# First graph of a graph-convolution kernel: x loaded transposed, centred and scaled from banks that TensorE fills

## The chip, the core and the metric

The kernel runs on one core of one Trainium2 chip. The metric is the device time of one execution in microseconds (us). A core has TensorE (PE in the profile; its weight loads are PEld), VectorE (DVE), ScalarE (ACT), GpSimd (POOL) and SyncE (SP), each with its own queue of instructions taken in order. They wait for each other by semaphores. Data lie in SBUF; TensorE writes to PSUM, of which this kernel uses eight banks of 128 partitions x 512 floats: `u_ps0` to `u_ps3` and `rot_ps0` to `rot_ps3`.

## The reference, cut to what matters

16 graphs, each with 512 nodes of 384 features. Before the two layers the features are normalised and clipped; this is the step that the change rewrites for the first graph.

```python
h = jnp.maximum(_layernorm(x, axis=-1), 0.0)       # (x - mean) / sqrt(var + 1e-5)
# per layer, on h of shape (B, 512, 384):
u = jnp.einsum('bid,bjd->bij', h, h) / temper
a = jax.nn.softmax(u, axis=-1)
delta = a * adjacency_matrix
attn = delta / (jnp.sum(delta, axis=-1, keepdims=True) + 1e-10)
hl, hs, hr = h @ wl.T + b_l, h @ ws.T + b_s, h @ wr.T + b_r
ctx = (attn * upper) @ hl + diag_a[..., None] * hs + (attn * lower) @ hr
o = relu((ctx - mean) / jnp.sqrt(var + LN_EPS) * g + beta)
# result: x + o of the second layer
```

## The kernel before

The graphs are worked in eight pairs. A pair has four steps: layer 0 of graph a and of graph b, then layer 1 of both. In each step TensorE makes the scores of four row tiles (`scores`, or `first_scores` in the very first step), twelve projections (`project`) and four attention products (`attend`). Every product of two fp32 matrices is made of three in a rounded format: each operand is split into a high part, which ScalarE rounds, and a low part, the difference, which VectorE or GpSimd subtracts (`ht_hi`/`ht_lo` for the features, `w_hi`/`w_lo` for the weights, `hw_hi`/`hw_lo` for the projections, `et_hi`/`et_lo` for the masked exponentials). The features are held transposed, with the 384 features in three blocks (KB = 3) of 128 partitions and the 512 nodes along the free dimension.

All orders are written out by hand, one program for each engine. From the second graph on, x comes to SBUF twice: by rows into `x_norm` (`load_stat_rows`), for VectorE's mean and variance, and transposed into `xt_sb` (`load_xt`). The mean and the reciprocal deviation of the 512 rows are written to a small tensor in DRAM and read back spread over 128 partitions (`store_x_rows`, `spread_x_rows`). GpSimd subtracts the mean (`x_centre`, L924), VectorE clips and scales (`x_scale`, L670), ScalarE rounds (`round_x`, L550) and VectorE subtracts the low part (`x_low`, L728).

The first graph goes another way, since nothing can hide it. Its x is loaded by rows in four pieces of 192 KB (L274, L488). VectorE makes the statistics (L615, L621, L625), GpSimd the reciprocal deviation (`x_rstd_of`, L917), VectorE the shift (L630). ScalarE and VectorE normalise two row tiles each in place (L479, L634). TensorE, which has worked off five products on zeros until then (L349), transposes twelve 128x128 blocks into three banks (L355). ScalarE clips and rounds each bank into `ht_hi` (L493) and VectorE takes the low part from the same bank (L645). `first_scores` begins with the first block of 128 features and waits for `ht_lo_done` once per block.

Beside this the first layer's weights are loaded in three chunks (L250), rounded by ScalarE (`round_w`, L485) and split by GpSimd (chunk 0, L932) and VectorE (chunks 1 and 2, L650). The first projection waits until all three are split. VectorE then goes on to the statistics of the second graph (`x_stats_of(1)`) and from there to the first step's evacuations (`evacuate`, L717) and masks (`mask`, L682, after ScalarE's exponential, L512). At the end of the first step GpSimd splits the first chunk of the second layer's weights (`split_w`, L937).

## Time and profile before

| | us |
|---|---|
| median of 3 runs | 1180.22 |
| lowest and highest | 1179.71, 1180.55 |
| the profiled execution's own time | 1179.74 |
| its span, first to last instruction | 1178.0 |
| TensorE busy | 1167.0 (99%) |
| VectorE, ScalarE, GpSimd busy | 939.7, 495.0, 639.4 |
| TensorE's share of the chain that ended last | 97% |

The profile comes from one execution, so durations and sums are made against its time; the 1.7 us between span and time lie outside the recorded instructions. TensorE's ends are modelled from starts and shapes. A wait is given as the idle time of an engine and the instruction that ended it. TensorE is the engine at the end of the chain for nearly the whole span; the other engines matter where it waits for them.

### The profile page before, as it was taken

How to read it: one execution, taken by the hardware profiler on the slowest of the kernel's cores; microseconds unless marked ns; L12 is line 12 of the kernel's file. 1: busy time of each engine (PE TensorE's matmuls, PEld its weight loads, DVE VectorE, ACT ScalarE, POOL GpSimd, SP SyncE). 2: the span in 40 equal slices, each digit the busy share in tenths (PEclk: the TensorE clock that was granted, in tenths of full speed). 3: DMA queues.
4: the chain of work that ended last, by engine and by line, in shares of the span. 5: the costliest groups of instructions: out<-in, count | busy, mean ns of one | idle time of the engine just before them, and what ended most of it. 6: DMA issues, size and time to landing. Idle time of an engine off the chain costs nothing.

```text
span 1178.0 us, 18565 instructions
## 1 busy us (share of the span) xinstructions
PE 1167.0 (99%) x6998; PEld 1158.1 (98%) x6998; DVE 939.7 (80%) x1872; ACT 495.0 (42%) x1065; POOL 639.4 (54%) x669
## 2 busy tenths in 40 slices
PE   9999999999999999999999999999999999999997
PEld 7999999999999999999999999999999999999997
DVE  6778986689866988769887598876988769875688
ACT  5346433364343543444334443344333454335532
POOL 4685463654635556445555456554475544754347
PEclk9999999999999999999999999999999999999999
DMA  7521312013121131211212112211212113110000
GB/s 245 187 66 55 116 55 81 22 52 117 55 81 37 36 117 55 81 37 62 91 55 81 37 68 85 67 68 37 88 66 81 55 36 113 41 54 1 1 28 27
DMA packets 43481, 80.55 MB, mean 68 GB/s; under 512 B 6912, under 2 KB 24832, under 8 KB 43392
## 3 DMA queue, kind: packets, MB, share of 16 engines
q1 hardware_dynamic: 43104, 78.98, 20.1%
q8 instruction: 55, 0.90, 0.3%
q10 hardware_dynamic: 288, 0.39, 0.1%
q14 instruction: 34, 0.28, 0.1%
HBM read 66.72 MB, written 12.64 MB: 67 GB/s over the span
## 4 chain that ended last, share of the span: by engine, by line
PE 97%; DVE 2%; issue 0%; DMA 0%; ACT 0%; POOL 0%; DVEq 0%
PE rot_ps L344 17%; PE rot_ps L343 17%; PE rot_ps L342 17%; PE u_ps L342 14%; PE u_ps L344 14%; PE u_ps L343 14%; PE rot_ps L405 2%; PE u_ps L398 2%; PE rot_ps L414 1%; DVE xt_sb L670 0%; DMA x_norm<-x_dram 0%; DVE hs L774 0%; DVE z L754 0%; DVE stats L780 0%; DVE x_stats L615 0%
## 5 line engine op out<-in xcount | busy, mean ns | idle before, releaser
L950 POOL TENSOR_TENSOR hw_lo<-proj,hw_hi 128x384 fp32r<-128x384 f32 x256 | 281.6, 1120 | 280.3 <-ACT hw_hi L530 280.3
L342 PE MATMUL rot_ps<-w_hi,ht_hi 128*128 128x384 f32 x1152 | 389.2, 338 | 0.0
L344 PE MATMUL rot_ps<-w_hi,ht_lo 128*128 128x384 f32 x1152 | 385.4, 335 | 0.0
L343 PE MATMUL rot_ps<-w_lo,ht_hi 128*128 128x384 f32 x1152 | 385.2, 334 | 0.0
L343 PEld LDWEIGHTS rot_ps<-w_lo,ht_hi 128*128 128x128 f32 x1152 | 216.5, 188 | 0.0
L342 PEld LDWEIGHTS rot_ps<-w_hi,ht_hi 128*128 128x128 f32 x1152 | 216.5, 188 | 0.0
L344 PEld LDWEIGHTS rot_ps<-w_hi,ht_lo 128*128 128x128 f32 x1152 | 216.2, 188 | 0.0
L505 ACT ACTIVATE u_off<-u_ps 128x128 f32<-128x128 f32 (+1 forms) x128 | 42.5, 332 | 393.7 <-PE u_ps L344 393.5
L717 DVE TENSOR_TENSOR proj<-rot_ps,bias 128x384 f32<-128x384 f32 x256 | 140.1, 550 | 47.4 <-PE rot_ps L344 45.7
L962 POOL TENSOR_TENSOR dg<-et_hi,tri 128x256 fp32r<-128x256 f32 x128 | 113.5, 887 | 94.5 <-PE u_ps L344 94.5
L530 ACT ACTIVATE hw_hi<-proj 128x384 fp32r<-128x384 f32 x256 | 127.9, 520 | 66.0 <-DVE proj L717 66.0
L342 PE MATMUL u_ps<-hw_hi,et_hi 128*128 128x386 f32 x384 | 131.8, 343 | 0.0
L774 DVE SCALAR_TENSOR_TENSOR hs<-hs,e_diag,u_ps 128x385 f32<-128x385 f32 x128 | 78.6, 614 | 66.2 <-PE u_ps L344 65.4
L687 DVE TENSOR_TENSOR et_lo<-e_sb,et_hi 128x512 fp32r<-128x512 f32 x128 | 130.6, 1029 | 0.0
L344 PE MATMUL u_ps<-hw_hi,et_lo 128*128 128x386 f32 x384 | 129.9, 338 | 0.0
L343 PE MATMUL u_ps<-hw_lo,et_hi 128*128 128x384 f32 x384 | 129.6, 337 | 0.0
L962 POOL TENSOR_TENSOR dg<-et_lo,tri 128x256 fp32r<-128x256 f32 x128 | 120.4, 941 | 0.0
L342 PE MATMUL u_ps<-ht_hi 128*128 128x256 f32 (+1 forms) x384 | 118.8, 309 | 1.2 <-DVE ht_lo L645 0.7
L344 PE MATMUL u_ps<-ht_hi,ht_lo 128*128 128x256 f32 (+1 forms) x384 | 118.8, 309 | 0.0
L343 PE MATMUL u_ps<-ht_lo,ht_hi 128*128 128x256 f32 (+1 forms) x384 | 118.3, 308 | 0.0
L967 POOL TENSOR_TENSOR rstd<-var_eps,minus_half 128x4 f32<-128x4 f32 (+1 forms) x35 | 38.7, 1105 | 124.3 <-DVE var_eps L741 123.9
L717 DVE TENSOR_TENSOR hs<-rot_ps,bias 128x384 f32<-128x384 f32 x128 | 67.0, 549 | 26.7 <-PE rot_ps L344 26.1
(89 smaller groups left out, 2038.7 us busy)
## 6 DMA issues: line engine op xcount, KB each, us to landing
out_dram<-z SPq DMA_DIRECT2D x64, 192.0 KB, 1.9
x_norm<-x_dram SPq DMA_DIRECT2D x15, 768.0 KB, 4.3
xt_sb<-x_t_dram SPq DMA_DIRECT2D x15, 768.0 KB, 4.5
adj_a<-adj_t_dram SPq DMA_DIRECT2D x8, 1024.0 KB, 5.4
adj_b<-adj_t_dram SPq DMA_DIRECT2D x8, 1024.0 KB, 5.4
x_norm<-rows_dram SPq DMA_DIRECT2D x15, 512.0 KB, 3.8
x_a<-x_dram SPq DMA_DIRECT2D x8, 768.0 KB, 4.6
x_b<-x_dram SPq DMA_DIRECT2D x8, 768.0 KB, 4.6
```

Of the source, the lines that this page charges most:

```text
L342: pe.matmul(dst, a_hi, b_hi, start=first and m == 0, stop=False)
L343: pe.matmul(dst[:, 0:b_lo.shape[1]], a_hi, b_lo, start=False, stop=False)
L344: done = pe.matmul(dst, a_lo, b_hi, start=False, stop=last and m == n - 1)
L398: done = pe.transpose(u_ps[t][:, column * P:(column + 1) * P], u_off[:, source * P:(source + 1) * P], ident[:, :])
L505: act.activation(u_off[:, OFF_AT[t] * P:OFF_AT[t] * P + width], u_ps[t][:, first_block * P:first_block * P + width], ACT.Copy).then_inc(of ...
L530: act.activation(hw_hi[:, t, n, 0:dim], proj[:, t % 2, n, :], ACT.Copy).then_inc(hw_hi_done, 1)
L687: dve.tensor_tensor(et_lo[:, i, :], e_sb[:, i, :], et_hi[:, i, :].bitcast(F32), ALU.subtract).then_inc(et_lo_done, 1)
L717: dve.tensor_tensor(dst, bank(it, s, "P", t, n)[:, 0:dim], bias[:, layer, n, :], ALU.add).then_inc(p_freed, 1)
L774: dve.scalar_tensor_tensor(out=hs[:, i, 0:dim + 1], in0=hs[:, i, 0:dim + 1], scalar=e_diag[:, i:i + 1], in1=u_ps[i][:, 0:dim + 1], op0=ALU ...
L950: pool.tensor_tensor(hw_lo[:, t, n, :], proj[:, t % 2, n, :], hw_hi[:, t, n, 0:dim].bitcast(F32), ALU.subtract).then_inc(hw_lo_done, 1)
L962: pool.tensor_tensor(dg[:, i % 2, part, :, :], block_t.unsqueeze(1).to_broadcast([P, 2, P]), tri[:, :, :], ALU.mult).then_inc(dg_done, 1)
L967: pool.tensor_tensor(rstd[:, cols], var_eps[:, cols], minus_half[:, cols], ALU.pow).then_inc(rstd_done, 1)
```

## The change

The first graph's x is now loaded twice, by rows for the statistics as before, and transposed into `xt_sb` right behind (one DMA of 768 KB, ahead of the weights in SP's queue). Normalising by rows, the shift and the twelve transposes of x are gone. In their place TensorE spreads the mean: four transposes of a broadcast column of `x_mv` fill bank `rot_ps1` so that every partition holds the 512 means, and four more fill `rot_ps2` with the reciprocal deviations. VectorE subtracts bank 1 from a block of `xt_sb` (`centre_first`), clips and multiplies by bank 2 (`scale_first`), ScalarE rounds the block from SBUF, and VectorE subtracts the rounded part, from SBUF too (`low_first`). ScalarE's rounding of the first weight chunk moves behind the first block's. The load of the second graph's rows waits for the first graph's statistics instead of its transposes, and that of its transposed x for the first graph's three low parts. The other edits renumber waits whose semaphores now count the first graph as well.

```diff
@@ -168,9 +167,7 @@
         ht_lo_done = sem("ht_lo_done")
         x_stats_done = sem("x_stats_done")
         x_rstd_done = sem("x_rstd_done")
-        x_shift_done = sem("x_shift_done")
-        x_norm_act_done = sem("x_norm_act_done")
-        x_norm_dve_done = sem("x_norm_dve_done")
+        x_first_spread = sem("x_first_spread")
         ones_done = sem("ones_done")
         stats_done = sem("stats_done")
         aggr_done = sem("aggr_done")
...
@@ -272,12 +268,14 @@
 
             for t in range(0, TILES, 2):
                 sp.dma_start(x_norm[:, t, :], rows(x, 0)[:, t, :]).then_inc(x_first[t], 16)
+            load_xt(0)
             for c in range(KB):
                 load_w(c)
             load_bias(0)
             sp.dma_start(adj_sb[0][:, :, :], rows(adj_t, 0)).then_inc(adj_loaded[0], 16)
-            sp.wait_ge(t_ready, KB)
+            sp.wait_ge(x_stats_done, TILES)
             load_stat_rows(1)
+            sp.wait_ge(ht_lo_done, KB)
             load_xt(1)
             sp.dma_start(gamma_t[:, :], ln_w0_t[:, :]).then_inc(col_loaded, 16)
             sp.dma_start(beta_t[:, :], ln_b0_t[:, :]).then_inc(col_loaded, 16)
...
@@ -294,7 +292,7 @@
             def pair(it, first, last):
                 next_a, next_b = it * 2 + 2, it * 2 + 3
                 if not last:
-                    sp.wait_ge(xt_scaled, KB * (next_a - 1))
+                    sp.wait_ge(xt_scaled, KB * next_a)
                     load_stat_rows(next_a)
                     sp.wait_ge(ht_lo_done, LEAD_T + at(it, 0, KB, N_H))
                     load_xt(next_a)
...
@@ -313,7 +311,7 @@
                     sp.wait_ge(w_lo1_done, KB)
                     sp.dma_start(x_sb[1][:, :, :], rows(x, 1)).then_inc(x_loaded[1], 16)
                 if not last:
-                    sp.wait_ge(xt_scaled, KB * next_a)
+                    sp.wait_ge(xt_scaled, KB * next_b)
                     spread_x_rows(next_b)
                 for g in range(2):
                     s = 2 + g
...
@@ -348,13 +346,16 @@
             for _ in range(5):
                 pe.matmul(rot_ps[0][:, :], diag_junk[:, 0, :], flat(diag_junk, 0, n_rows), start=True, stop=True)
             pe.wait_ge(consts, 8)
-            pe.wait_ge(x_norm_dve_done, TILES - X_ACT)
-            pe.wait_ge(x_norm_act_done, X_ACT)
-            for db in range(KB):
+            def spread_first(q):
                 for t in range(TILES):
-                    done = pe.transpose(rot_ps[(db - KB) % ROT][:, t * P:(t + 1) * P],
-                                        x_norm[:, t, db * P:(db + 1) * P], ident[:, :])
-                done.then_inc(t_ready, 1)
+                    done = pe.transpose(rot_ps[1 + q][:, t * P:(t + 1) * P],
+                                        x_mv[:, 0, q, t:t + 1].to_broadcast([P, P]), ident[:, :])
+                done.then_inc(x_first_spread, 1)
+
+            pe.wait_ge(x_stats_done, 2 * TILES)
+            spread_first(0)
+            pe.wait_ge(x_rstd_done, 1)
+            spread_first(1)
 
             def step(it, s, first, last):
                 final = last and s == STEPS - 1
...
@@ -473,12 +474,6 @@
 
         @block.scalar
         def _(act):
-            def x_normalise_first():
-                act.wait_ge(x_shift_done, 1)
-                for t in range(X_ACT):
-                    act.activation(x_norm[:, t, :], x_norm[:, t, :], ACT.Identity, bias=x_shift[:, t:t + 1],
-                                   scale=x_mv[:, 0, 1, t:t + 1]).then_inc(x_norm_act_done, 1)
-
             def round_w(c):
                 layer, kb = chunks[c]
                 act.wait_ge(w_loaded[c], 16)
...
@@ -486,11 +481,11 @@
 
             for t in range(1, TILES, 2):
                 act.dma_start(x_norm[:, t, :], rows(x, 0)[:, t, :]).then_inc(x_first[t], 16)
-            x_normalise_first()
-            round_w(0)
             for db in range(KB):
-                act.wait_ge(t_ready, db + 1)
-                act.activation(ht_hi[:, 0, db, :], rot_ps[(db - KB) % ROT][:, :], ACT.Relu).then_inc(ht_hi_done, 1)
+                act.wait_ge(xt_scaled, db + 1)
+                act.activation(ht_hi[:, 0, db, :], xt_sb[:, db, :], ACT.Copy).then_inc(ht_hi_done, 1)
+                if db == 0:
+                    round_w(0)
             for c in range(1, KB):
                 round_w(c)
 
...
@@ -544,13 +539,13 @@
 
                 def round_x(db):
                     graph = it * 2 + (1 if s == 0 else 2)
-                    act.wait_ge(xt_scaled, KB * (graph - 1) + (db + 1))
+                    act.wait_ge(xt_scaled, KB * graph + (db + 1))
                     if s == 2 and db == 0:
                         act.wait_ge(p_ready, at(it, s, 3 * TILES, N_P))
                     act.activation(ht_hi[:, graph % 2, db, :], xt_sb[:, db, :], ACT.Copy).then_inc(ht_hi_done, 1)
 
                 def round_h(db):
-                    act.wait_ge(t_ready, LEAD_T + at(it, s, db + 1, N_HT))
+                    act.wait_ge(t_ready, at(it, s, db + 1, N_HT))
                     src, parity = bank(it, s, "T", db)[:, :], 1 - s % 2
                     if db == 0:
                         act.wait_ge(hw_lo_done, at(it, s, 2 * TILES, EIGHT))
...
@@ -625,26 +620,37 @@
                 dve.tensor_scalar(x_var_eps[:, :], x_mv[:, graph % 2, 1, :], 1e-5, None,
                                   ALU.add).then_inc(x_stats_done, 1)
 
-            def x_normalise_first():
-                dve.wait_ge(x_rstd_done, 1)
-                dve.scalar_tensor_tensor(out=x_shift[:, :], in0=x_mv[:, 0, 0, :], scalar=-1.0, in1=x_mv[:, 0, 1, :],
-                                         op0=ALU.mult, op1=ALU.mult).then_inc(x_shift_done, 1)
-                dve.wait_ge(x_shift_done, 1)
-                for t in range(X_ACT, TILES):
-                    dve.tensor_scalar(x_norm[:, t, :], x_norm[:, t, :], x_mv[:, 0, 1, t:t + 1], x_shift[:, t:t + 1],
-                                      ALU.mult, ALU.add).then_inc(x_norm_dve_done, 1)
+            def centre_first(db):
+                dve.tensor_tensor(xt_sb[:, db, :], xt_sb[:, db, :], rot_ps[1][:, :],
+                                  ALU.subtract).then_inc(xt_centred, 1)
+
+            def scale_first(db):
+                dve.wait_ge(xt_centred, db + 1)
+                dve.scalar_tensor_tensor(out=xt_sb[:, db, :], in0=xt_sb[:, db, :], scalar=0.0, in1=rot_ps[2][:, :],
+                                         op0=ALU.max, op1=ALU.mult).then_inc(xt_scaled, 1)
+
+            def low_first(db):
+                dve.wait_ge(ht_hi_done, db + 1)
+                dve.tensor_tensor(ht_lo[:, 0, db, :], xt_sb[:, db, :], ht_hi[:, 0, db, :].bitcast(F32),
+                                  ALU.subtract).then_inc(ht_lo_done, 1)
 
             dve.memset(diag_junk[:, :, :], 0.0).then_inc(zeros_done, 1)
             for t in range(TILES):
                 dve.wait_ge(x_first[t], 16)
                 x_statistics(t)
             x_variance(0)
-            x_normalise_first()
-            for db in range(KB):
-                dve.wait_ge(ht_hi_done, db + 1)
-                dve.scalar_tensor_tensor(out=ht_lo[:, 0, db, :], in0=rot_ps[(db - KB) % ROT][:, :], scalar=0.0,
-                                         in1=ht_hi[:, 0, db, :].bitcast(F32), op0=ALU.max,
-                                         op1=ALU.subtract).then_inc(ht_lo_done, 1)
+            dve.wait_ge(x_first_spread, 1)
+            dve.wait_ge(xt_loaded, 16)
+            centre_first(0)
+            centre_first(1)
+            dve.wait_ge(x_first_spread, 2)
+            scale_first(0)
+            scale_first(1)
+            low_first(0)
+            centre_first(2)
+            scale_first(2)
+            low_first(1)
+            low_first(2)
             for c in range(1, KB):
                 dve.wait_ge(w_hi_done, c + 1)
                 dve.tensor_tensor(w_lo[:, 0, c, :], w_stages[c], w_hi[:, 0, c, :].bitcast(F32),
...
@@ -666,7 +672,7 @@
 
                 def x_scale(graph, db):
 
-                    dve.wait_ge(xt_centred, KB * (graph - 1) + (db + 1))
+                    dve.wait_ge(xt_centred, KB * graph + (db + 1))
                     dve.scalar_tensor_tensor(out=xt_sb[:, db, :], in0=xt_sb[:, db, :], scalar=0.0, in1=rstd_b,
                                              op0=ALU.max, op1=ALU.mult).then_inc(xt_scaled, 1)
 
...
@@ -918,7 +924,7 @@
                                    ALU.pow).then_inc(x_rstd_done, 1)
 
             def x_centre(graph):
-                pool.wait_ge(xt_loaded, 16 * graph)
+                pool.wait_ge(xt_loaded, 16 * (graph + 1))
                 pool.wait_ge(x_rows_spread, 16 * graph)
                 for db in range(KB):
                     pool.tensor_tensor(xt_sb[:, db, :], xt_sb[:, db, :], mean_b, ALU.subtract).then_inc(xt_centred, 1)
```

In the first rows of TensorE's queue (rot_ps0 to rot_ps3 are the banks, diag_junk the zeros) there stands before:

```order
L349 MATMUL rot_ps0<-diag_junk 128x512 [waits zeros_done]
L349 MATMUL rot_ps0<-diag_junk 128x512 x4
L355 MATMUL rot_ps1<-ident,x_norm 128x128 [waits x_norm_act_done,x_norm_dve_done,consts]
L355 MATMUL rot_ps1<-ident,x_norm 128x128 x3
L355 MATMUL rot_ps2<-ident,x_norm 128x128 x4
L355 MATMUL rot_ps3<-ident,x_norm 128x128 x4
L342 MATMUL u_ps0<-ht_hi 128x384 [waits ht_lo_done]
```

and in the changed kernel, whose line numbers differ by a few:

```order
L347 MATMUL rot_ps0<-diag_junk 128x512 [waits zeros_done]
L347 MATMUL rot_ps0<-diag_junk 128x512 x4
L351 MATMUL rot_ps1<-ident,x_mv 128x128 [waits x_stats_done,consts]
L351 MATMUL rot_ps1<-ident,x_mv 128x128 x3
L351 MATMUL rot_ps2<-ident,x_mv 128x128 [waits x_rstd_done]
L351 MATMUL rot_ps2<-ident,x_mv 128x128 x3
L340 MATMUL u_ps0<-ht_hi 128x384 [waits ht_lo_done]
```

Eight small transposes of statistics take the place of twelve of x; both sets stand behind the same five products on zeros.

VectorE's queue between the first graph's variance and the second graph's statistics, before (x_mv holds mean and variance, w_lo the low weights):

```order
L625 TENSOR_SCALAR x_var_eps<-x_mv 128x4 [waits x_stats_done]
L630 SCALAR_TENSOR_TENSOR x_shift<-x_mv 128x4 [waits x_rstd_done]
L634 TENSOR_SCALAR x_norm<-x_norm,x_mv,x_shift 128x384 [waits x_shift_done]
L634 TENSOR_SCALAR x_norm<-x_norm,x_mv,x_shift 128x384
L645 SCALAR_TENSOR_TENSOR ht_lo<-rot_ps1,ht_hi 128x512 [waits ht_hi_done]
L645 SCALAR_TENSOR_TENSOR ht_lo<-rot_ps2,ht_hi 128x512 [waits ht_hi_done]
L645 SCALAR_TENSOR_TENSOR ht_lo<-rot_ps3,ht_hi 128x512 [waits ht_hi_done]
L650 TENSOR_TENSOR w_lo<-z,w_hi 128x1152 [waits w_hi_done]
L650 TENSOR_TENSOR w_lo<-x_b,w_hi 128x1152 [waits w_hi_done]
L615 BN_STATS x_stats<-x_norm 128x6 [waits consts,x_norm_loaded,zeros_done,w_lo0_done]
```

and after:

```order
L620 TENSOR_SCALAR x_var_eps<-x_mv 128x4 [waits x_stats_done]
L624 TENSOR_TENSOR xt_sb<-xt_sb,rot_ps1 128x512 [waits xt_loaded,x_first_spread]
L624 TENSOR_TENSOR xt_sb<-xt_sb,rot_ps1 128x512
L629 SCALAR_TENSOR_TENSOR xt_sb<-xt_sb,rot_ps2 128x512 [waits xt_centred,x_first_spread]
L629 SCALAR_TENSOR_TENSOR xt_sb<-xt_sb,rot_ps2 128x512 [waits xt_centred]
L634 TENSOR_TENSOR ht_lo<-xt_sb,ht_hi 128x512 [waits ht_hi_done]
L624 TENSOR_TENSOR xt_sb<-xt_sb,rot_ps1 128x512
L629 SCALAR_TENSOR_TENSOR xt_sb<-xt_sb,rot_ps2 128x512 [waits xt_centred]
L634 TENSOR_TENSOR ht_lo<-xt_sb,ht_hi 128x512 [waits ht_hi_done] x2
L656 TENSOR_TENSOR w_lo<-z,w_hi 128x1152 [waits w_hi_done]
L656 TENSOR_TENSOR w_lo<-x_b,w_hi 128x1152 [waits w_hi_done]
```

Six operations on 512 columns are new on VectorE ahead of the weights' low parts, and the three low parts of the features now read two tensors of SBUF where they read a bank and one tensor.

ScalarE's queue at the same place, before:

```order
L479 ACTIVATE x_norm<-x_norm,x_shift,x_mv 128x384 [waits x_shift_done]
L479 ACTIVATE x_norm<-x_norm,x_shift,x_mv 128x384
L485 ACTIVATE w_hi<-e_sb 128x1152 [waits w_loaded_0]
L493 ACTIVATE ht_hi<-rot_ps1 128x512 [waits t_ready]
L493 ACTIVATE ht_hi<-rot_ps2 128x512 [waits t_ready]
L493 ACTIVATE ht_hi<-rot_ps3 128x512 [waits t_ready]
L485 ACTIVATE w_hi<-z 128x1152 [waits w_loaded_1]
```

and after:

```order
L486 ACT_TABLE_LOAD
L486 ACTIVATE ht_hi<-xt_sb 128x512 [waits xt_scaled]
L480 ACTIVATE w_hi<-e_sb 128x1152 [waits w_loaded_0]
L486 ACTIVATE ht_hi<-xt_sb 128x512 [waits xt_scaled] x2
L480 ACTIVATE w_hi<-z 128x1152 [waits w_loaded_1]
```

The rounding of the first weight chunk (`w_hi<-e_sb`, which GpSimd's split waits for) has moved from ahead of the three feature blocks to between the first and the second.

## Rows read from the trace of the kernel before

**Rows 1.** Waits of TensorE, whole run: waited for, us in total, times, longest.

```profile
PE rot_ps L349 <- DVE diag_junk L637: 1.5, 1, 1.5
PE u_ps L342 <- DVE ht_lo L645: 0.7, 1, 0.7
PE u_ps L342 <- DVE ht_lo L728: 0.5, 1, 0.5
PE rot_ps L355 <- ACT x_norm L479: 0.4, 1, 0.4
```

**Rows 2.** Chain that ended last, its beginning: start us, us, what.

```profile
6.84 1.05 POOL x_mv L917
...
10.98 0.70 DVE ht_lo L645
...
11.73 0.44 PE u_ps L342
```

**Rows 3.** Timeline of TensorE and its weight loads: start us, us, instruction.

```profile
6.78 0.34 PEld L349 LDWEIGHTS rot_ps<-diag_junk 128*128 128x128 f32 x1 [0.52 <-issue]
7.63 0.24 PEld L349 LDWEIGHTS rot_ps<-diag_junk 128*128 128x128 f32 x1 [0.52 <-issue]
8.11 0.19 PEld L349 LDWEIGHTS rot_ps<-diag_junk 128*128 128x128 f32 x1 [0.24 <-issue]
...
9.56 1.50 PE L355 MATMUL rot_ps<-ident,x_norm 128*128 128x128 f32 x12 [0.43 <-ACT x_norm L479]
...
13.60 0.34 PE L342 MATMUL u_ps<-ht_hi 128*128 128x384 f32 x1
...
17.11 0.34 PE L342 MATMUL rot_ps<-w_hi,ht_hi 128*128 128x384 f32 x1
```

**Rows 4.** Timeline of the other engines, 10 to 21 us.

```profile
10.55 2.67 POOL L932 TENSOR_TENSOR w_lo<-e_sb,w_hi 128x1152 fp32r<-128x1152 f32 x1 [2.67 <-ACT w_hi L485]
...
10.98 1.89 DVE L645 SCALAR_TENSOR_TENSOR ht_lo<-rot_ps,ht_hi 128x512 fp32r<-128x512 f32 x3 [2.00 <-ACT ht_hi L493]
...
14.35 1.34 DVE L650 TENSOR_TENSOR w_lo<-x_b,w_hi 128x1152 fp32r<-128x1152 f32 x1
17.46 1.94 DVE L615 BATCH_NORM_STATS2 x_stats<-x_norm 128x6 f32<-128x384 f32 x4 [1.76 <-DMA x_norm<-x_dram]
...
19.93 0.56 DVE L717 TENSOR_TENSOR proj<-rot_ps,bias 128x384 f32<-128x384 f32 x1
20.40 0.68 DVE L682 TENSOR_TENSOR e_sb<-u_ps,adj_a 128x512 f32<-128x512 f32 x1
...
19.53 0.58 ACT L512 ACTIVATE u_ps<-u_ps 128x512 f32<-128x512 f32 x1 [1.94 <-PE u_ps L398]
```

**Rows 5.** Groups by line and shape, whole run: count, busy us, mean ns, idle before.

```profile
L687 DVE TENSOR_TENSOR et_lo<-e_sb,et_hi 128x512 fp32r<-128x512 f32 x128 | 130.6, 1029 | 0.0
...
L550 ACT ACTIVATE ht_hi<-xt_sb 128x512 fp32r<-128x512 f32 x45 | 26.4, 625 | 52.8 <-DVE xt_sb L670 52.8
```

**Rows 6.** GpSimd's split beside VectorE (timeline); L728 over the run: min/median/max ns.

```profile
43.89 2.66 POOL L937 TENSOR_TENSOR w_lo<-x_b,w_hi 128x1152 fp32r<-128x1152 f32 x1
...
44.36 2.74 DVE L728 TENSOR_TENSOR ht_lo<-xt_sb,ht_hi 128x512 fp32r<-128x512 f32 x1
...
L728 DVE TENSOR_TENSOR ht_lo<-xt_sb,ht_hi x45: 678/684/2736, 42.5 to 1057.4; 128x512 fp32r<-128x512 f32 x45
```

**Rows 7.** Two weight DMAs: issue in SP's timeline; then KB, us to landing.

```profile
1.69 0.42 SPq L250 DMA_DIRECT2D e_sb<-w_t_dram  x1
2.16 0.43 SPq L250 DMA_DIRECT2D z<-w_t_dram  x1
...
e_sb<-w_t_dram SPq DMA_DIRECT2D x1, 576.0 KB, 5.1
z<-w_t_dram SPq DMA_DIRECT2D x1, 576.0 KB, 6.2
```

**Rows 8.** Busy time by engine, 27 to 46 us, with counts; granted clock, DMA.

```profile
27.00:46.00 19.00, 19.00 (x111) 19.00 (x110) 16.03 (x22) 5.22 (x9) 19.00 (x17) 1.00 0.62 221
```

2 lines of the change are left out of this document (removed).

## The prediction

> **What bounds the kernel now.** I read the view of waits first, for TensorE over the whole run. It has four entries [rows 1]: 1.5 us until its first operand, 0.4 us for the normalised x before the opening transposes, 0.7 us for the first `ht_lo`, and 0.5 us for an `ht_lo` of the second graph (L728). Behind those TensorE is fed to the end. So the kernel ends when TensorE has done a fixed amount of work, and a change in the first graph's preparation counts only by what it does to the start of the first scores, now 11.73 us, and to stalls behind it. The chain of waits gives the way to that start [rows 2]: GpSimd's reciprocal deviation is there at 7.89, VectorE's first `ht_lo` runs from 10.98, the first score at 11.73. In the timeline TensorE is not free all that time [rows 3]. The five opening products on zeros are ten passes of 512 columns. Their weight loads come 0.85 us apart up to 7.63 (the lower of the two clock levels, 1.2 GHz) and 0.48 us apart there (2.4 GHz), although the profile's clock column grants 1.00 throughout. The last pass starts about 0.43 us after the load at 8.11 and streams for 0.43 us, so the engine is free at about 8.97. Before, this cost nothing: the transposes waited for ScalarE until 9.5 anyway.
>
> **Edits with one answer.** The shift, two ScalarE normalisations, two on VectorE and twelve transposes go. The renumbered waits (`xt_scaled`, `xt_centred`, `xt_loaded`, `t_ready`) only count the first graph's increments too, which costs nothing in steady state. SP's queue issues one DMA more, so the seven behind it are issued some 0.45 us later.
>
> **The load of x transposed.** It stands ahead of the weights in SP's queue. The second weight block was issued at 2.16 and landed 6.2 us later, at 8.36, when 0.79 MB of x and 1.18 MB of weights had moved [rows 7]. The transposed x needs 0.79 + 0.79 MB moved, less than that, so I take about 7.3 and at most 8.4. Nothing wants it before 9.6: free. If that cover were gone, each late microsecond would be one. The two weight blocks landed 1.57 us apart for 0.59 MB, 375 GB/s, so 0.79 MB delays what lies behind by 2.1 us. The first weights then land near 8.9, wanted at 12.0. The second graph's x for its statistics, which ended VectorE's wait at 17.46 [rows 4], lands near 19.5. Its issue moved ahead (it now waits for the statistics, about 6.2), but the queue is full until then.
>
> **The start of the first scores.** The spreads stand behind the opening products. Twelve transposes took 1.50 us, 0.112 us each and 0.27 us the last [rows 3], so the mean's bank is full at 8.97 + 0.34 + 0.27 = 9.58 and the other at 10.03, both later than their data (about 6.6 and 7.89). VectorE is not shown subtracting a bank from SBUF at this size. The nearest rows are the mask on a bank, 0.68 us long, and the old `ht_lo`, three in 1.89 us, one every 0.60 [rows 4]. I take 0.60 from start to start and 0.68 for the last; the ends would be 0.5 and 0.7, for the sum some 0.3 us either way. Two centrings start at 9.60 and 10.20, the first scaling runs 10.80 to 11.48. ScalarE's copy of a 128x512 block of SBUF takes 0.63 us on average [rows 5]: 12.13. `low_first(0)` ends at 12.83, the scores start at 12.88. That is **1.15 us later** than 11.73.
>
> **The second block.** Block 0 of the scores takes 13.60 − 11.73 = 1.87 us [rows 3], so TensorE wants `ht_lo` of block 1 at 14.75. In the new order ScalarE rounds the first weights between `ht_hi` 0 and 1 (1.15 us, 12.05 to 13.20), and then GpSimd splits them, 13.20 to 15.87, if it takes its 2.67 us [rows 4]. VectorE does centring 2 (12.75), scaling 2 (13.45) and wants `low_first(1)` at about 14.05. Before, this subtraction read a bank: it ran beside the same GpSimd split at full speed (10.98 against 10.55) [rows 4]. Now both of its inputs lie in SBUF. The trace has that pair once: GpSimd's split of other weights from 43.89 for 2.66 us, VectorE's `ht_lo` from SBUF at 44.36 for 2.74 us, where the median of 45 such is 0.68 [rows 6]. It ended 0.55 us behind the split, so it did nothing until the split was over. By that row `low_first(1)` ends at 15.87 + 0.55 = 16.42 and TensorE goes on at 16.47, where it was at 13.60: **2.87 us later**, 1.72 of it a new stall.
>
> The mean of 128 `et_lo` subtractions beside shorter GpSimd work is 1.03 us [rows 5], which could be read as a slowdown by half instead: the subtraction would end near 15.1 and TensorE be 1.5 us late. The Trainium skill (SBUF — State Buffer, section SBUF: two separate sides) says that the port pair of VectorE and GpSimd is an exclusive lock for a whole instruction, taken by a VectorE operation with two SBUF inputs against a GpSimd one that reads SBUF. By that rule the sum is the 2.87 above, by the other reading about 1.5; the row at 44.36 agrees with the rule.
>
> **Behind the scores.** Blocks 1 and 2 take 17.11 − 13.60 = 3.51 us: first projection at 19.98. It waits for all first low weights. VectorE has `ht_lo` 2 done at 17.05 and then two splits of 1.34 us [rows 4], done at about 19.65: 0.3 us to spare. VectorE's statistics of the second graph follow, from 19.65 (data at 19.5). Before, 2.47 us passed from their start to the first evacuation, 17.46 to 19.93: now 22.1, or 2.2 late. But the first mask waits for ScalarE's first exponential, which follows TensorE's mirrors, so it moves from 19.53 to 22.41, ends 0.58 later, and the mask starts at 23.03 where it started at 20.40: 2.63 late [rows 4]. Evacuations, rounding and GpSimd's lower parts follow that by 2.63 us. GpSimd is busy for all 19 us from 27 to 46 [rows 8], so it brings this lateness to the split at 43.89 and the `ht_lo` behind it, for which TensorE waits 0.5 us [rows 1, 6]. TensorE comes there 2.87 late, GpSimd 2.63: the stall shrinks from 0.5 to about 0.3, and all that follows is **2.6 us late**. Its floor, with the stall gone, is 2.87 − 0.5 = 2.4; if GpSimd were as late as TensorE, 2.9.
>
> **The sum.** Span 1178.0 + 2.6 = 1180.6; the profiled execution took 1179.74 and would take 1182.4. It lies 0.5 under the median 1180.22, from which the forecast is **1182.8 us**. With 0.3 for VectorE's steps and 0.3 for the floor, its own range is 1182.1 to 1183.5.
>
> **Rivals.**
> - *VectorE is not held by GpSimd* (20%). If `low_first(1)` ends by about 15.1, by sharing or by coming first, no long stall appears. TensorE is 1.2 to 1.5 late, the low weights about 1.9 at worst: 1181.5 to 1182.1, say 1181.9, not slower by more than can be told. It decides at about 15.2 us. For it: the margin between 13.20 and 14.05 is only 0.85 us, and the 1.03 us rows. Against it: the 2.74 us row.
> - *The chain gets shorter as the words of the change suggest* (7%). If the opening products ended before the data came (the clock rising sooner), the banks would be full at 7.2 and 8.5, the scores would start near 10.6, 1.2 early. But the split then runs about 10.9 to 13.6 and `low_first(1)` ends at 14.1 against 13.60 before: 0.5 late, 1180.8. To be faster by 0.2% it would have to gain 2.4 us, more than this start plus the later stall (1.7) can give.
> - *TensorE's clock falls* (13%). It would work 1 us between 9 and 12.9 and wait again at 14.75. At the lower level a pass takes 0.85 instead of 0.43 us [rows 3]. The first block's loss hides in the new stall; behind 16.47 the loss is half of the slow time. At the start it took about 6 us of work before the clock rose, so from 16.5 it stays low until 19 to 22.5: 1.3 to 3 us more, 1183.9 to 1185.8, say 1184.8. For it: 4.5 of these 6.5 us are idle. Against it: 1.1 us idle before the old start left the pitch at the upper level. The Trainium skill (TensorE: Matmul & The Clock Gate, section What's actually happening) says that the throttled state is the default and activity releases it; that a gap of this size is enough to bring it back no run here shows.
>
> **How the numbers follow.** Forecast 60%, rivals 20, 7 and 13%. A run of this kernel can tell about 0.2% (2.4 us), so slower means above 1182.6: of the forecast's 60 some 42 points, and all 13 of the clock: 55% slower. Same: 18 + 20 + 5: 43%. Faster 2%. The range 1180.9 to 1184.6 takes in forecast, the first rival and part of the others.
>
> **What the changed profile would show.** The mean's spread starts at 9.0, behind the zeros' products, not at 6.6. First score at 12.9. `low_first(1)` is over 2 us long and ends 0.55 behind GpSimd's first split; TensorE has a new wait of about 1.7 us for it. The wait at L728's counterpart near 50 us is 0.2 to 0.5. A `low_first(1)` of 0.7 us, a start before 12 or score passes at twice the pitch would each prove a step wrong, as would VectorE waiting for the transposed x.

## The result, and the profile after

The changed kernel takes **1184.14 us** (median of 8 runs, 1182.12 to 1184.60), the kernel before 1179.91 in the 8 runs made beside them (1179.71 to 1180.57). The ratio is 1.0029, 95% interval 1.0020 to 1.0039. It is slower, as forecast, and inside the stated range. It is 1.3 us above the predicted time, and beyond the forecast's own range of 1182.1 to 1183.5. The profiled execution took 1184.05 with a span of 1182.3, 4.3 more than before.

TensorE's waits answer to [rows 1] (waited for, us in total, times, longest):

```profile
PE u_ps L340 <- DVE ht_lo L634: 3.8, 2, 2.9
PE rot_ps L347 <- DVE diag_junk L637: 1.5, 1, 1.5
PE u_ps L340 <- DVE ht_lo L734: 0.5, 1, 0.5
```

The wait for the first graph's `ht_lo` grew from 0.7 to 3.8 us in two pieces, and the wait in the second graph (L728 before, L734 now) is still 0.5. So all 4.3 us arise before the first projection, the first product that needs the weights. The timeline of TensorE shows where (start us, us, instruction, idle before it and its releaser), beside [rows 3]:

```profile
1.50 6.98 PE L347 MATMUL rot_ps<-diag_junk 128*128 128x512 f32 x10 [1.50 <-DVE diag_junk L637]
8.32 1.04 PE L351 MATMUL rot_ps<-ident,x_mv 128*128 128x128 f32 x8
12.28 0.44 PE L340 MATMUL u_ps<-ht_hi 128*128 128x384 f32 x1 [2.93 <-DVE ht_lo L634]
...
15.90 0.69 PE L340 MATMUL u_ps<-ht_hi 128*128 128x384 f32 x1 [0.83 <-DVE ht_lo L634]
...
21.39 0.34 PE L340 MATMUL rot_ps<-w_hi,ht_hi 128*128 128x384 f32 x1
```

The first score is 0.55 us later than before (12.28 for 11.73), the second block 2.30 later (15.90 for 13.60), the first projection 4.28 later (21.39 for 17.11). The last step, from 2.30 to 4.28, is blocks 1 and 2 taking 5.49 us instead of 3.51. The windows of 2 us say why (busy us and count of each engine, then PEclk, DMA share, GB/s):

```profile
12.00:14.00 2.00, 1.72 (x8) 1.72 (x9) 1.97 (x4) 1.50 (x3) 1.36 (x1) 0.81 0.87 123
14.00:16.00 2.00, 1.17 (x7) 0.87 (x5) 2.00 (x2) 2.00 (x3) 1.30 (x1) 0.50 0.95 333
16.00:18.00 2.00, 2.00 (x7) 2.00 (x8) 2.00 (x3) 0.32 (x1) 0.00 (x0) 0.50 1.05 426
18.00:20.00 2.00, 2.00 (x10) 2.00 (x10) 0.99 (x1) 0.00 (x0) 0.00 (x0) 0.50 1.02 352
20.00:22.00 2.00, 2.00 (x15) 2.00 (x14) 0.59 (x2) 1.30 (x4) 0.00 (x0) 0.99 0.52 175
```

Here the granted clock falls to 0.50, the 1.2 GHz level, at about 13.3 us and comes back at about 20. In TensorE's weight loads it is the step from 0.19 to 0.33 us:

```profile
13.09 0.19 PEld L342 LDWEIGHTS u_ps<-ht_hi,ht_lo 128*128 128x128 f32 x1
13.27 0.33 PEld L340 LDWEIGHTS u_ps<-ht_hi 128*128 128x128 f32 x1
```

They are back at 0.19 at 20.16. Ahead of the fall TensorE had done 1.04 us of small transposes, idled 2.93 us and worked about 1 us on the scores.

The other engines, VectorE's and GpSimd's timelines, answer to [rows 4]:

```profile
8.96 1.28 DVE L624 TENSOR_TENSOR xt_sb<-xt_sb,rot_ps 128x512 f32<-128x512 f32 x2 [2.30 <-PE rot_ps L351]
10.16 1.28 DVE L629 SCALAR_TENSOR_TENSOR xt_sb<-xt_sb,rot_ps 128x512 f32<-128x512 f32 x2
11.54 0.69 DVE L634 TENSOR_TENSOR ht_lo<-xt_sb,ht_hi 128x512 fp32r<-128x512 f32 x1
...
13.46 2.99 DVE L634 TENSOR_TENSOR ht_lo<-xt_sb,ht_hi 128x512 fp32r<-128x512 f32 x2
...
21.41 1.94 DVE L610 BATCH_NORM_STATS2 x_stats<-x_norm 128x6 f32<-128x384 f32 x4 [2.42 <-DMA x_norm<-x_dram]
...
24.60 0.69 DVE L688 TENSOR_TENSOR e_sb<-u_ps,adj_a 128x512 f32<-128x512 f32 x1 [0.17 <-ACT u_ps L507]
```

```profile
12.64 2.67 POOL L938 TENSOR_TENSOR w_lo<-e_sb,w_hi 128x1152 fp32r<-128x1152 f32 x1 [4.86 <-ACT w_hi L480]
```

The subtraction of the second block of features ends at 15.86 (the chain of waits gives it from 13.55 for 2.31), 0.55 us behind the end of GpSimd's split at 15.31. And a second thing is late: the second graph's statistics start at 21.41, 3.95 us later than 17.46, still ended by their rows' DMA.

SP's issues and the DMAs' times to landing (KB, us) answer to [rows 7]:

```profile
1.69 0.43 SPq L257 DMA_DIRECT2D xt_sb<-x_t_dram  x1
2.16 0.49 SPq L246 DMA_DIRECT2D e_sb<-w_t_dram  x1
...
5.69 0.64 SPq L275 DMA_DIRECT2D adj_a<-adj_t_dram  x1
6.37 2.30 SPq L254 DMA_DIRECT2D x_norm<-x_dram  x1
```

```profile
adj_a<-adj_t_dram SPq DMA_DIRECT2D x1, 1024.0 KB, 13.7
xt_sb<-x_t_dram SPq DMA_DIRECT2D x1, 768.0 KB, 6.9
x_norm<-x_dram SPq DMA_DIRECT2D x1, 768.0 KB, 14.9
e_sb<-w_t_dram SPq DMA_DIRECT2D x1, 576.0 KB, 7.8
```

The added load lands at 8.6, just ahead of its use at 8.96. The cover is thin: in two kernels below whose orders are the same up to there (rows first, and all three remedies) VectorE's first centring is released by this load and not by the spread, some 0.2 us after the spread was full. The first weights land at 9.96 (before: 1.69 + 5.1 = 6.79, [rows 7]), the second graph's rows at 6.37 + 14.9 = 21.3.

### The profile page after: what moved, and what is told of

Read it like the earlier page. It is cut to its first block, busy times and chain, and to the rows that moved or that the text cites. A ratio compares the mean times of both kernels' runs of the same rounds, so it can differ in the third digit from the quotient of the medians.

```text
span 1182.3 us, 18561 instructions
## 1 busy us (share of the span) xinstructions
PE 1168.7 (99%) x6994; PEld 1160.3 (98%) x6994; DVE 943.9 (80%) x1875; ACT 495.1 (42%) x1063; POOL 639.1 (54%) x669
## 4 chain that ended last, share of the span: by engine, by line
PE 97%; DVE 2%; issue 0%; ACT 0%; DVEq 0%
PE rot_ps L342 17%; PE rot_ps L340 17%; PE rot_ps L341 17%; PE u_ps L340 14%; PE u_ps L342 14%; PE u_ps L341 14%; PE rot_ps L406 2%; PE u_ps L399 2%; PE rot_ps L415 1%; PE rot_ps L347 1%; DVE xt_sb L676 0%; DVE ht_lo L634 0%; DVE hs L780 0%; DVE z L760 0%; DVE stats L786 0%
```

## Experiments

The experiments look for up to three causes: VectorE held by GpSimd's split (1.7 us in the sum), TensorE's fallen clock (2 us), and the rows of the second graph coming late behind the added load. The recorded expectations call it theory A that only TensorE's own delay counts and the rows are no limit, and theory B that the rows are a second limit beside it. A third question is whether the rows are late because of the second graph's transposed x and not because of the first's.

Each run is described against the changed kernel unless it says otherwise. "Before" is the kernel before, run between them on the same chip: 1180.23, 1180.32 and 1180.15 us in the three sets (31, 32 and 27 runs; the third set, from the section on what beats both, is from another chip). Each profile is of one execution. Those of the fill and of the banks are the fastest of their 11, so their spans say less than their medians.

### Filling TensorE's gap

Three more products on zeros behind the spreads, so that TensorE does not idle there:

```diff
             spread_first(1)
+            for _ in range(3):
+                pe.matmul(rot_ps[0][:, :], diag_junk[:, 0, :], flat(diag_junk, 0, n_rows), start=True, stop=True)
```

> The changed kernel with three more products on zeros behind the two spreads (2.6 us at 2.4 GHz, until about 11.9), so that TensorE is busy until the first scores and its clock should stay at the upper level. Nothing else differs. Both theories: start of the scores still near 12.3, VectorE's subtraction of the second block still held until 0.55 us behind GpSimd's split, scores restart near 15.9, first projection near 19.4 instead of 21.4. Theory A (the clock alone is what my forecast missed): the 2 us reach the end, 1182.1 us. Theory B (the second graph's rows, which land at 21.3, are a second limit of the same size): VectorE's first evacuation stays at about 23.9, GpSimd's chain stays 3.9 us late, TensorE's wait before the second step grows from 0.5 to about 2.2 us, and the time is 1183.8 us.

Measured: **1182.87** (1182.59 to 1183.52, 11 runs; 1.0021, 1.0012 to 1.0030). The clock stays at 1.00, and the first projection is at 19.11 (+2.00). But the waits show what took over, as does the start of the statistics in VectorE's timeline:

```profile
PE u_ps L340 <- DVE ht_lo L636: 1.9, 2, 1.6
...
PE u_ps L340 <- DVE ht_lo L736: 1.4, 1, 1.4
```

```profile
20.46 1.94 DVE L612 BATCH_NORM_STATS2 x_stats<-x_norm 128x6 f32<-128x384 f32 x4 [1.88 <-DMA x_norm<-x_dram]
```

TensorE gained 2.28 us at the first projection, and 0.9 of it went into the wait before the second graph. Of the 2.28 us the clock's fall is 1.88: blocks 1 and 2 take 3.61 us here (15.50 to 19.11) for 5.49. The other 0.40 us is an earlier first score (11.88 for 12.28), which the edit does not reach; the table below takes it up. The span is 2.9 over that of before, as are the statistics (3.00). So the clock cost real time, and the rows cap what its removal gives: theory A's 1182.1 is too low, and theory B's growing wait is seen, with the rows landing earlier and the time lower than its 1183.8.

### Scaled blocks in PSUM

The scaled blocks are written to free PSUM banks instead of back to `xt_sb`, so the subtraction again reads one bank and one tensor of SBUF:

```diff
-                act.activation(ht_hi[:, 0, db, :], xt_sb[:, db, :], ACT.Copy).then_inc(ht_hi_done, 1)
+                act.activation(ht_hi[:, 0, db, :], (rot_ps[0], rot_ps[3], rot_ps[1])[db][:, :], ACT.Copy).then_inc(ht_hi_done, 1)
...
+            scaled = [rot_ps[0], rot_ps[3], rot_ps[1]]
...
-                dve.scalar_tensor_tensor(out=xt_sb[:, db, :], in0=xt_sb[:, db, :], scalar=0.0, in1=rot_ps[2][:, :],
+                dve.scalar_tensor_tensor(out=scaled[db][:, :], in0=xt_sb[:, db, :], scalar=0.0, in1=rot_ps[2][:, :],
...
-                dve.tensor_tensor(ht_lo[:, 0, db, :], xt_sb[:, db, :], ht_hi[:, 0, db, :].bitcast(F32),
+                dve.tensor_tensor(ht_lo[:, 0, db, :], scaled[db][:, :], ht_hi[:, 0, db, :].bitcast(F32),
```

> The changed kernel, but the scaled blocks are written to three PSUM banks instead of back to SBUF, and ScalarE's rounding and VectorE's subtraction read those banks. The subtraction then reads one SBUF tensor only. Theory of exclusion (VectorE waits for GpSimd's split only where both its inputs lie in SBUF): the subtraction of the second block takes 0.7 us instead of 2.4 beside the same split, the second block of scores starts at 14.9, directly behind the first. Rival (any VectorE work is slowed beside the split): it still takes 2 us or more. The clock still falls near 13.3 since the idle time ahead of the start is unchanged. Time: 1183.1 us if nothing else limits (1.0 us gained), 1183.8 if the second graph's rows at 21.3 do (0.3 gained).

Measured: **1182.92** (1181.88 to 1183.88, 11 runs; 1.0021, 1.0012 to 1.0030). VectorE's and GpSimd's timelines:

```profile
12.59 1.45 DVE L636 TENSOR_TENSOR ht_lo<-rot_ps,ht_hi 128x512 fp32r<-128x512 f32 x2
```

```profile
11.76 2.65 POOL L940 TENSOR_TENSOR w_lo<-e_sb,w_hi 128x1152 fp32r<-128x1152 f32 x1 [4.03 <-ACT w_hi L480]
```

Two subtractions take 1.45 us in the midst of the split, where they took 2.99. TensorE's wait in the middle of the scores is gone, and the first projection is at +1.24. The clock still falls, but not near 13.3 as I had expected (same columns as above):

```profile
10.00:12.00 2.00, 0.59 (x2) 0.59 (x3) 1.90 (x5) 1.97 (x3) 0.24 (x1) 0.88 0.96 374
12.00:14.00 2.00, 2.00 (x9) 2.00 (x8) 1.93 (x3) 1.46 (x3) 2.00 (x1) 0.50 0.33 115
14.00:16.00 2.00, 2.00 (x12) 2.00 (x11) 1.64 (x3) 1.42 (x2) 0.41 (x1) 0.76 1.00 354
```

The weight loads go to 0.31 us at 11.52, 0.1 us after the first score, and are back at 0.19 at 14.99: 3.4 us at the lower level. The statistics start 2.25 us late and the span is 2.2 over. In this profile the chain that ended last runs through the load of the second graph's rows (13.57 us from 6.02) and their statistics.

### Is it the second graph's transposed x?

The filled kernel, with SP issuing the second graph's transposed x only when the rows have landed:

```diff
             sp.wait_ge(ht_lo_done, KB)
+            sp.wait_ge(x_norm_loaded, 16)
             load_xt(1)
```

> As the run with three more products on zeros, and the second graph's transposed x is loaded only once its rows have landed. Theory B: the rows land near 19.5 instead of 21.3, since they no longer share the queue with the transposed x; VectorE's evacuations come 2.1 to 2.6 us later than in the kernel before instead of 3.9, and the time is 1182.2 to 1182.5 us, what the forecast said without the clock and with rows at 19.5. Theory A (the load is no limit): same as the run without this edit.

Measured: **1182.98** (1182.32 to 1183.75, 11 runs), the same as the filled kernel. In its profile the statistics start at 20.09, where 19.5 was expected of theory B and the filled kernel has 20.46. A miss: issued 4 us later, that load moved the rows by 0.4 us at most.

These three edits together (the fill, now in `u_ps[0]`, the banks, the late transposed x):

> All three edits: products on zeros behind the spreads (into a bank of the scores), scaled blocks in banks, second transposed x behind the rows. TensorE starts the scores at 12.3, has no second wait there and reaches the projections at 17.7, 0.6 us later than the kernel before. Theory B: the rows at 19.5 still make VectorE and GpSimd 2 us late, the wait before the second step is about 1.9 us, 1181.8 us. If the rows are no limit: 1180.6 us.

Measured: **1183.58** (1182.20 to 1184.19, 9 runs; 1.0016 to 1.0035), a miss of 1.8. TensorE was almost in time, yet nothing was gained over the fill alone. VectorE's timeline, then TensorE's waits:

```profile
20.53 1.94 DVE L613 BATCH_NORM_STATS2 x_stats<-x_norm 128x6 f32<-128x384 f32 x4 [3.00 <-DMA x_norm<-x_dram]
```

```profile
PE u_ps L341 <- DVE ht_lo L739: 1.7, 1, 1.7
...
PE u_ps L341 <- POOL dg L973: 0.3, 1, 0.3
PE u_ps L341 <- POOL hw_lo L961: 0.3, 1, 0.3
```

First projection 17.59 (+0.48), statistics +3.07, span +3.0. Here the late rows hold the kernel, through VectorE and GpSimd.

### The load alone

This time the kernel **before**, with the added load and nothing that uses it (the wait keeps the buffer's two loads in order, and GpSimd's wait for the buffer, not shown, counts one load more):

```diff
+            load_xt(0)
             for c in range(KB):
...
             load_stat_rows(1)
+            sp.wait_ge(xt_loaded, 16)
             load_xt(1)
```

> The kernel before with nothing but the added load: the first graph's transposed x goes into its tile ahead of the weights, nobody uses it, and the second graph's transposed x waits for it. Theory (the queue is full until the second graph's rows are in, so 0.79 MB ahead delays them by about 2 us): rows land near 19.5 instead of 17.4, the first evacuation moves from 19.9 to about 22, and the time is 1182.2 us; the first weights may land after 9.4 too and delay ScalarE by up to 0.6. Rival (free time of the queue between 10 and 13 us takes up the load): 1180.2 us.

Measured: **1182.60** (1182.05 to 1183.59, 11 runs; 1.0019, 1.0010 to 1.0028). The first projection stands at 17.02, where before it was 17.11. VectorE's timeline and TensorE's waits:

```profile
20.70 1.94 DVE L617 BATCH_NORM_STATS2 x_stats<-x_norm 128x6 f32<-128x384 f32 x4 [5.08 <-DMA x_norm<-x_dram]
```

```profile
PE u_ps L344 <- DVE ht_lo L730: 1.6, 1, 1.6
...
PE u_ps L344 <- POOL hw_lo L952: 0.8, 1, 0.8
```

A load that nobody uses costs 2.3 us (1182.60 for 1180.32), in a kernel whose TensorE is on time until 17 us.

### The rows first

SP issues the second graph's rows ahead of the biases and the adjacency. These now stand behind the wait for the statistics, so the adjacency is issued at 7.77 us instead of 5.69:

```diff
-            load_bias(0)
-            sp.dma_start(adj_sb[0][:, :, :], rows(adj_t, 0)).then_inc(adj_loaded[0], 16)
             sp.wait_ge(x_stats_done, TILES)
             load_stat_rows(1)
+            load_bias(0)
+            sp.dma_start(adj_sb[0][:, :, :], rows(adj_t, 0)).then_inc(adj_loaded[0], 16)
```

> The changed kernel with one move in SP's queue: the second graph's rows are loaded ahead of the three biases and the adjacency instead of behind them. Nothing on TensorE, VectorE or ScalarE differs. The rows should land near 15 us, so VectorE's statistics follow its weight splits without a wait. Theory (two limits of the same size, the late rows and TensorE's own delay by the held subtraction and the lower clock): taking the rows away as a limit changes the time by at most 0.3 us, 1183.8 to 1184.1, and the wait before the second step shrinks to zero only if GpSimd comes earlier than TensorE. Rival (the rows are the one limit): about 1181.5 us.

Measured: **1182.06** (10 runs; 1.0011 to 1.0030), but in two groups: six runs of 1181.13 to 1182.09 and four of 1183.99 to 1184.67. The profiled run is of the lower group (1181.84). Its windows:

```profile
12.00:13.00 1.00, 0.97 (x4) 0.98 (x5) 0.96 (x2) 0.82 (x2) 0.62 (x1) 0.68 0.95 376
13.00:14.00 1.00, 1.00 (x5) 1.00 (x4) 1.00 (x2) 0.68 (x2) 1.00 (x1) 0.50 1.18 306
14.00:15.00 1.00, 1.00 (x7) 1.00 (x5) 1.00 (x1) 1.00 (x2) 1.00 (x1) 0.50 0.89 138
15.00:16.00 1.00, 0.69 (x4) 0.40 (x4) 1.00 (x2) 1.00 (x2) 0.03 (x1) 0.61 0.97 217
16.00:17.00 1.00, 1.00 (x8) 1.00 (x7) 1.00 (x2) 0.06 (x1) 0.00 (x0) 1.00 0.99 360
```

The lower level lasts from about 12.4 to 15.8, half as long as in the changed kernel, and lies mostly on block 0, whose lateness the held subtraction hides. First projection +2.21, span +2.1. I read the upper group as runs with the long stay. It is 2.8 us higher by the medians of the groups. No run of it was profiled, but the mean granted clock of every run is on record: 0.997 in all six of the lower group, 0.995 in all four of the upper. The changed kernel shows the like, 0.995 in its five runs from 1184.05 up and 0.996 in the three below (1182.12, 1182.57, 1183.41). Over 1182 us a mean lower by 0.002 is 2.4 us of full speed, 1.2 to 3.5 with the rounding. So the upper group ran longer at the lower level; that it did so at this place is not shown, and the long stay of the profile above cost 1.9 us and not 2.8. Of what was expected, one group fits each theory.

The same with the fill:

> Rows ahead of biases and adjacency, and three more products on zeros behind the spreads, so that the clock stays at the upper level. What is left is the late start and the subtraction held by GpSimd's split: TensorE 2.3 us late at the first projection, GpSimd's chain no later than that, the wait before the second step 0.5 us or less. This is what the forecast described: 2.3 to 2.6 us over the kernel before, about 1182.6 us, against 1182.9 with the late rows. If the rows were the limit of the run with the products alone, this one is faster than it by 0.3 to 0.7 us; if not, the two are equal.

Measured: **1182.11** (1181.19 to 1182.51, 11 runs; 1.0007 to 1.0024). The clock is at 1.00, there is no upper group, TensorE is 2.58 late at the first projection and the span 2.5. It is 0.8 us faster than the fill alone, which is what was expected if the rows were that kernel's limit, and 0.5 below the 1182.6 that I gave it. With clock and rows both out of the way, the later start (12.45) and the held subtraction are left. And all three remedies together (fill, banks, rows first):

> Rows ahead of biases and adjacency, products on zeros behind the spreads, scaled blocks in banks. All three causes are taken away and only the later start of the scores (about 0.3 us, 12.0 against 11.7) is left. Theory of three causes: 1180.2 to 1180.9 us, level with the kernel before. If a cause is missing, it stays over 1182.

Measured: **1180.53** (1179.53 to 1181.19, 11 runs; ratio 1.0000, 0.9991 to 1.0009). Its waits:

```profile
PE u_ps L340 <- DVE ht_lo L638: 0.5, 1, 0.5
PE u_ps L340 <- DVE ht_lo L738: 0.5, 1, 0.5
```

With the three causes gone the changed kernel is level with the kernel before; the start, at 12.28, is still not earlier in this profile. The moved adjacency has become the next thing waited for:

```profile
21.36 0.69 DVE L692 TENSOR_TENSOR e_sb<-u_ps,adj_a 128x512 f32<-128x512 f32 x1 [0.40 <-DMA adj_a<-adj_t_dram]
```

### One table of the profiles

All in us later than in the profile of before; each row from that kernel's own timeline, waits and span. The last column is from all runs: the median over that of before in the same set.

| kernel | first score | first projection | second graph's statistics | wait before the second graph (0.5 before) | span | median |
|---|---|---|---|---|---|---|
| changed | 0.55 | 4.28 | 3.95 | 0.5 | 4.3 | 4.2 |
| fill | 0.15 | 2.00 | 3.00 | 1.4 | 2.9 | 2.6 |
| banks | -0.32 | 1.24 | 2.25 | 1.4 | 2.2 | 2.7 |
| fill, late second x | -0.16 | 1.70 | 2.63 | 1.3 | 2.6 | 2.8 |
| fill, banks, late second x | 0.19 | 0.48 | 3.07 | 1.7 | 3.0 | 3.4 |
| before, with the load | -0.08 | -0.09 | 3.24 | 1.6 | 2.9 | 2.3 |
| rows first | 0.30 | 2.21 | 1.30 | 0.5 | 2.1 | 1.7 |
| fill, rows first | 0.72 | 2.58 | 1.73 | 0.5 | 2.5 | 1.8 |
| fill, banks, rows first | 0.55 | 0.84 | 0.47 | 0.5 | 0.8 | 0.2 |

In each row the span follows the larger of the columns for the projection and the statistics, to within 0.35 us. There are two chains, and in these nine profiles the end follows the later.

The first score moves by 1.04 us between profiles whose orders are the same up to the spreads (11.41 with the banks, 12.45 in the fill with the rows first). It follows the opening products on zeros, whose weight loads stand 0.43 us apart from 4.90 us on in the one and from 6.76 in the other. The first scores, with the banks and then with the fill and the rows first:

```profile
11.41 0.60 PE L340 MATMUL u_ps<-ht_hi 128*128 128x384 f32 x1 [2.90 <-DVE ht_lo L636]
```

```profile
12.45 0.44 PE L340 MATMUL u_ps<-ht_hi 128*128 128x384 f32 x1 [0.35 <-DVE ht_lo L636]
```

So when the clock rises at the start, which no edit here sets, moves the start of the changed kernel by a microsecond. It does not move that of the kernel before, whose transposes wait for the normalised x: the loads there speed up at 7.63 and, with the unused load, at 5.60, and the first scores stand at 11.73 and 11.65. What an edit did to TensorE behind the start is therefore read from the second column less the first: 3.73 in the changed kernel, 1.85 with the fill (the clock: 1.88), 0.29 with the fill and the banks (the held subtraction: 1.6), and 1.91 with the rows first, so that the short stay at the lower level cost next to nothing there.

### What beats both

The wait of 0.5 us before the second graph hangs on GpSimd: it splits the second step's weights while VectorE wants to subtract [rows 6]. In the kernel before, I put that split behind the first step's reciprocal deviation, and ScalarE's first weight rounding behind the first `ht_hi`:

```diff
             x_normalise_first()
-            round_w(0)
...
+                if db == 0:
+                    round_w(0)
...
-                if first and s == 0:
-                    split_w(KB)
...
                 rstd_of(slice(0, TILES), 1)
+                if first and s == 0:
+                    split_w(KB)
```

> The kernel before with two moves: ScalarE rounds the first weights behind the first block of features instead of ahead of it, and GpSimd's split of the second layer's first weights stands behind the first step's reciprocal deviation instead of ahead of it. If ScalarE's 1.15 us (9.3 to 10.5, transposes ready at 10.2) and the split (44.63 to 47.02 on the chain) are what holds those two places, the start comes 0.2 to 0.3 us earlier and the wait of 0.5 us at 47 us is gone: 1179.5 us. If VectorE's other work sets the second wait, 1180.0.

Measured: **1179.22** (1178.89 to 1179.44, 11 runs; 0.9990, 0.9982 to 0.9999) against 1180.15: 0.9 us less. The wait in the second graph is gone. That is the split's move: the first score is 0.08 us earlier and the first projection 0.12 later, so the other move gave nothing. The runs also lie closer, within 0.55 us where those of before spread over 1.55. The same later split in the repaired changed kernel (fill, banks, rows first), and there with four opening products instead of five:

```diff
-            for _ in range(5):
+            for _ in range(4):
                 pe.matmul(rot_ps[0][:, :], diag_junk[:, 0, :], flat(diag_junk, 0, n_rows), start=True, stop=True)
```

> The run with all three causes removed, plus GpSimd's split of the second layer's first weights behind the first step's reciprocal deviation. The last wait of TensorE before the second step (0.5 us) goes: 1180.0 us against 1180.5.

> As the run before, with four opening products on zeros instead of five, so that the spreads start when their data are there. The mean's bank is full near 7.6 and the transposed x, landing between 7.6 and 8.9, becomes the last thing that the first centring waits for: scores start 0.3 to 0.8 us earlier, 1179.4 us. If the lower clock comes back because fewer products run at the start, up to 2.6 us are lost in some executions.

Measured: **1179.72** (0.9988 to 1.0005) and **1179.69** (0.9986 to 1.0004), 11 runs each. Both are level with before, the second 0.3 above what I expected of it. With one product fewer the first score stands at 11.83 for 12.03, and no time is gained that can be told. No version of the change that was run overtakes the kernel before with the same small repair.

## Why the prediction was right, and where it was off

- **What bounds the kernel: right, and incomplete.** The end moved with the start of the scores and the stalls behind it. But I let one chain set the end. There are two, TensorE's and that of the second graph's rows, and the second has far less slack than I gave it.
- **The start of the first scores: mechanism right, 0.6 too late.** I forecast 12.88 and it is 12.28. The spreads do stand behind the products on zeros, and start at 8.32 and not at 8.97, because in this execution the clock rose more than a pass earlier (weight loads 0.43 us apart from 6.60, where [rows 3] has 7.63). I took the kernel before's moment of that rise as fixed; the profiles have the first score from 11.41 to 12.45 by it. The 10.6 of the rival of a shorter chain (7%) was reached in none. VectorE's steps of 0.60 and ends of 0.68 were right to 0.05 us.
- **The second block: right.** Split of 2.67 us, subtraction held until 0.55 us behind its end, by the one row of [rows 6]. It came 0.56 early (15.86 for 16.42), all of it from the start. The rival of an unheld subtraction (20%) is out, and the banks show the cause: with one operand in PSUM the same two subtractions take 1.45 us beside the same split. The Trainium skill (SBUF — State Buffer, section SBUF: two separate sides) calls the pair an exclusive lock, and for VectorE names two SBUF inputs as the condition; both halves of that rule agree with these runs (2.99 us for the pair of subtractions with two SBUF inputs, 1.45 with one).
- **TensorE's clock: the step that failed.** I gave its fall 13% and it happened, at 13.3 us, for 6.8 us. Of this block 0's share hides in the stall, as I wrote, and about 1.9 us come on top (blocks 1 and 2 take 5.49 us, for 3.61 with the fill and 3.51 before). That is the term missing from my sum. The rival's price, 1.3 to 3 us, was right; its chance was not. The evidence that I set against it, 1.1 us of idling before the old start that did no harm, was too far from the new case of 1.04 us of small transposes between gaps, the second of 2.93 us. The Trainium skill (TensorE: Matmul & The Clock Gate, section What's actually happening) says that the throttled state is the default and activity releases it; these runs agree, since the extra products on zeros (six passes, 2.7 us) kept the clock at 1.00 in all the profiles that had them (each shows 1.00 in every window up to 22 us).
- **Behind the scores: the rows were under-sized.** I let the added 0.79 MB delay what lies behind it by 2.1 us, its size by 375 GB/s. In the profile above the first weight block was 3.17 late (9.96 for 6.79) and the rows 3.95 (21.41 for 17.46). In that execution the added load itself took 6.9 us to land. In five other profiles with the load in the same place (fill, banks, both with the late second x, before with the load) it took 5.9 to 6.1, the first weights landed in 6.8 to 7.0, which is 2.2 to 2.4 late and near my figure, and the rows landed 2.3 to 3.3 late. So the size by the rate holds for what stands right behind the load, and is mostly too small for the rows at the end of the queue; why is not shown. The kernel before with the unused load has its statistics 3.24 late. I had written "free" for the load because its own user was in time, and did not carry the delay of the rows to the end as a limit of its own.
- **The stall before the second graph: wrong.** It was to shrink from 0.5 to 0.3. GpSimd and VectorE became as late as TensorE (mask 24.60 for 20.40, +4.20; TensorE +4.28), so it stayed. This case was in my bounds (the 2.9).
- **The sum.** Forecast 2.6 of the span, measured 4.3. Difference 1.7: the blocks behind the stall +2.0 (1.9 of it the clock), the start −0.6, and +0.2 for the stall that did not shrink come to 1.6. The late rows add nothing to this sum since TensorE was as late as they; without the fallen clock they would have set the end at about +2.9, as the fill shows, so the forecast of 2.6 would have been 0.3 short for their sake.
- **The range** held because it reached into the rival of the clock (1183.9 to 1185.8; its low end should read 1182.8 + 1.3 = 1184.1), of which the result is the cheap end. That the median lies inside is in part luck: the early start took 0.6 us off, and 1184.14 + 0.6 would be outside the 1184.6. The forecast's own 1182.1 to 1183.5 is also 0.1 to 0.2 us wider than its terms of 0.3 give. The lateness of the rows lay beside TensorE's, not behind it: moving the rows alone left four of ten runs at 1184.0 to 1184.7.

**What stays open.** Why the lower clock level lasts now 3.4 us (banks, rows first) and now 6.8: the Trainium skill (TensorE: Matmul & The Clock Gate, section What's actually happening) ties the level to how busy the engine has been recently, and no run here shows what set the length. Why the added load lands now 5.9 and now 7.2 us after its issue, with the queue ahead of it the same. The rows vary too: the statistics start at 19.71 to 21.41 us with one order of SP's queue up to them. And why the three edits without the rows' move run slower in the median (1183.58) than the fill alone (1182.87): their profiled run, 1182.71, was one of the faster ones, and all nine have a mean granted clock of 0.998 or 0.999, so it is not the clock.

## What to carry to other kernels

A load put at the head of a queue is priced at its last dependent, not its first: list every transfer behind it with the time at which its user waits, and take that slack off. When a chain on TensorE is shortened to little work between gaps, look at what keeps its clock up, and price the fall as a case of its own. And two limits that are late together hide one another: removing the clock's fall gave TensorE 1.9 us behind the start and the kernel 1.3 by the medians, so take both away before you judge either. One profile is one execution: here the start moved by up to 1 us between executions, as much as some of the edits, so compare stretches that begin after it, and set the medians beside them.

## What the runs showed of the hardware that I had not expected

- After 1.04 us of small transposes and 2.93 us without work TensorE's granted clock fell to 0.50, about 1 us **after** work had come back (first score 12.28, fall 13.3), and stayed for 6.8 us, most of them at full load. In the run with the rows first it stayed 3.4 us, and with the banks it fell 0.1 us after the first score (11.41) and stayed 3.4 us. The runs with the rows first lie in two groups 2.8 us apart, with a mean granted clock of 0.997 in the one and 0.995 in the other.
- The opening products on zeros start at 1.50 us in every profile, and their weight loads come at the pitch of the upper level from 4.90 us in one execution and from 7.63 in another. This moves the first score of the changed kernel (11.41 to 12.45) and not that of the kernel before.
- An unused load of 0.79 MB ahead in SP's queue made a transfer issued at 11.02 us, 9.3 us after it, land 3.3 us later (20.6 for 17.3), though about 2.1 us would have moved its bytes at 375 GB/s.
- One issue of SP's took 2.30 us (6.37, with ten DMAs issued ahead on that queue), where its neighbours took 0.43 to 0.74. In the other profiles with that order it took 1.56 to 1.80, and 0.33 where the rows were the seventh.
- In both kernels the DMA rate falls for some 2 us near 12 (123 GB/s in the window 12 to 14 above; before at 10 to 12), about when the first bias rows land; with the rows moved ahead the low stretch is later (138 GB/s at 14 to 15). What causes it was not tested.
